# Second cross attention of a two-layer decoder: key tiles in runs of 4, 4, 4, 5 where they went 4, 4, 3, 3, 3

## What is computed

```python
def _L1_xattn_ref(x, latents, key_padding_mask, kv_gate, ...):   # x: ctx (4,1601,256), latents (4,512,256)
    x = layernorm(x, gamma_media, beta_media)
    latents = layernorm(latents, gamma_lat, beta_lat)
    kv = jnp.concatenate((x, latents * kv_gate), axis=1)          # 2113 rows
    q = (latents @ Wq).reshape(b, n, HEADS, DIM_HEAD)             # 8 heads of 64
    k = (kv @ Wk).reshape(b, f + n, HEADS, DIM_HEAD)
    v = (kv @ Wv).reshape(b, f + n, HEADS, DIM_HEAD)
    sim = jnp.einsum('bqhd,bkhd->bhqk', q * SCALE, k)
    sim = sim - jax.lax.stop_gradient(jnp.max(sim, axis=-1, keepdims=True))
    sim = jnp.where(valid_full[:, None, None, :], sim, NEG_INF)
    attn = jax.nn.softmax(sim, axis=-1)
    out = jnp.einsum('bhqk,bkhd->bqhd', attn, v).reshape(b, n, HEADS * DIM_HEAD)
    return out @ Wout
```

## Time and profile before

| | us |
|---|---|
| median of 3 runs | 2297.67 |
| lowest, highest | 2291.8, 2297.82 |
| the profiled execution | 2294.18 |
| its span, first to last instruction | 2292.4 |
| the stage that is touched | about 931 to 1930 in that span |
| granted PE clock over the span (share of full) | 0.944 |

### The profile page before, as it was taken

The page is one execution under the profiler, slowest core; times in us unless marked ns, Lnnn a source line. Parts: engine busy times, 40 slices in busy tenths (PEclk is TensorE's granted clock), DMA queues, the critical chain, the costliest instruction groups (busy, mean ns, idle before and its releaser), DMA issues. The chain is left out here.

```text
span 2292.4 us, 35767 instructions
## 1 busy us (share of the span) xinstructions
PE 2004.5 (87%) x12692; PEld 1395.7 (61%) x12692; DVE 1529.4 (67%) x2457; ACT 1158.6 (51%) x2226; POOL 954.7 (42%) x754
## 2 busy tenths in 40 slices
PE   7898867994989996899999999999999996799992
PEld 4565546993343544566666666665666664699992
DVE  5677864553787887688788778877888886222224
ACT  3332311102367456668775877677776772233332
POOL 2233232322221131166665756575666664222223
PEclk9999978997999997999999999999999997899996
DMA  4100016311000000100000000000000001621113
GB/s 156 39 23 22 23 64 258 101 63 62 0 0 1 0 29 27 40 1 1 30 1 1 10 29 1 1 10 1 1 1 1 10 1 65 250 75 36 38 33 120
DMA packets 36779, 93.30 MB, mean 41 GB/s; under 512 B 5479, under 2 KB 24443, under 8 KB 31998
## 3 DMA queue, kind: packets, MB, share of 16 engines
q1 hardware_dynamic: 30526, 74.72, 9.1%
q0 software_dynamic: 6080, 16.29, 2.1%
HBM read 76.56 MB, written 14.44 MB: 40 GB/s over the span
## 5 line engine op out<-in xcount | busy, mean ns | idle before, releaser
L2052 POOL TENSOR_TENSOR x_total<-x_total,x_pt 128x1024 f32<-128x1024 f32 x189 | 446.5, 2363 | 171.4 <-ACT x_pt L2138 153.6
L2160 ACT ACTIVATE x_pt<-PS,x_maskf 128x512 f32<-128x512 f32 x544 | 332.1, 689 | 165.0 <-PE PS L2474 163.6
L2259 DVE TENSOR_TENSOR PS<-x_pt,PS 128x512 f32<-128x512 f32 x480 | 333.5, 695 | 64.8 <-ACT x_pt L2160 27.3
L2277 DVE TENSOR_TENSOR x_pt<-x_pt,PS 128x1024 f32<-128x1024 f32 x320 | 320.4, 1053 | 0.7 <-PE PS L2492 0.7
L2474 PE MATMUL PS<-x_qs,x_ks 64*128 64x256 f32 x2176 | 281.9, 396 | 1.5 <-ACT x_pt L2160 1.5
L2451 PE MATMUL PS<-x_pt,x_vs 128*64 128x256 f32 x2108 | 262.7, 388 | 20.6 <-issue 12.1
L2138 ACT ACTIVATE x_pt<-x_pt 128x1536 f32<-128x1536 f32 (+1 forms) x160 | 266.5, 1667 | 12.8 <-DVE x_pt L2277 12.8
L2474 PEld LDWEIGHTS PS<-x_qs,x_ks 64*128 64x128 f32 x2176 | 199.6, 189 | 64.5 <-issue 39.0
L1143 PEld LDWEIGHTS PS<-m_xT,m_own 128*128 128x128 f32 x1984 | 234.5, 195 | 6.9 <-DVE m_own L1219 2.9
L1143 PE MATMUL PS<-m_xT,m_own 128*128 128x128 f32 x1984 | 235.4, 278 | 2.8 <-DVE m_own L1219 2.4
L2451 PEld LDWEIGHTS PS<-x_pt,x_vs 128*64 128x64 f32 x2108 | 141.8, 137 | 137.2 <-issue 67.5
(11 more groups left out here) (301 smaller groups left out, 2832.1 us busy)
## 6 DMA issues: line engine op xcount, KB each, us to landing
f_w<-in_L_ffn_w SPq DMA_DIRECT2D x32, 1024.0 KB, 6.5
a_ctxT<-in_ctxT SPq DMA_DIRECT2D x8, 800.5 KB, 4.3
f_w<-ys SPq DMA_DIRECT2D x24, 256.0 KB, 5.4
l_w<-in_ctx SPq DMA_DIRECT2D x4, 1024.0 KB
l_w<-in_L_attn_w SPq DMA_DIRECT2D x6, 512.0 KB, 7.6
a_xT<-in_xT SPq DMA_DIRECT2D x4, 512.0 KB, 5.8
X<-in_x SPq DMA_DIRECT2D x1, 2048.0 KB, 11.1
xr<-a_xn SPq DMA_DIRECT2D x16, 128.0 KB, 1.7
```

The lines of the kernel that those rows point to most:

```text
L2052: ins = nc.gpsimd.tensor_tensor(total2[:], first, tile[:, 2 * k + 2:2 * k + 4, :], ALU.add)
L2160: nc.scalar.activation(pt[:, s % 2, t, :].rearrange("p (h n) -> p h n", h=2), PS[:, first:first + 2, half], ACT.Identity, bias=maskf[:, b ...
L2259: ins = nc.vector.tensor_tensor(acc, tile, acc, ALU.max)
L2277: nc.vector.tensor_tensor(p_, p_, PS[:, MB, None, :].to_broadcast([P, at.stop - at.start, SPAN]), ALU.subtract).then_inc(lowered, 1)
```

## The change

The steps become four, with 4, 4, 4 and 5 tiles. The fills of keys and values no longer follow the runs: they have boundaries of their own (`CUTS`), 4, 4, 4, 4 and 1 tiles, so there are still five K and five V fills. The fifth K fill (one tile) is made in step 1 of an even slot, the fifth V fill (one tile) in step 3 of an even slot, both behind `weigh`. The fourth K fill is made where the fifth was. The pieces that DVE lowers are eight of two tiles and one of one tile, where they were seven of two and three of one. N fills, ten in slots i = 5 and 6, go 1, 2, 1, 1 and 1, 1, 2, 1 to a step (`TURNS`), where each step had one. O goes to steps 1 and 2 where it had 2 and 4; x and L stay in steps 1 and 3. The statistics are spread over 11 steps where it was 14, and ACT's normalising over 9 steps.

```diff
-    NG = 5
-    EDGES = [0, 4, 8, 11, 14, KT]
+    NG = 4
+    EDGES = [0, 4, 8, 12, KT]
+    CUTS = [0, 4, 8, 12, 16, KT]
+    NF = len(CUTS) - 1
+    FILLED = [range(CUTS[i], CUTS[i + 1]) for i in range(NF)]
...
-    PIECES = [(0, 2), (2, 4), (4, 6), (6, 8), (8, 10), (10, 11), (11, 13), (13, 14), (14, 16), (16, KT)]
+    PIECES = [(0, 2), (2, 4), (4, 6), (6, 8), (8, 10), (10, 12), (12, 14), (14, 16), (16, KT)]
...
-    SUMMED = [1, 3, 5, 6, SUMS]
+    SUMMED = [1, 3, 5, SUMS]
...
+        TURNS = {(0, 0): 1, (0, 1): 2, (0, 2): 1, (0, 3): 1, (1, 0): 1, (1, 1): 1, (1, 2): 2, (1, 3): 1}
+        BEFORE = {at: sum(n for other, n in TURNS.items() if other < at) for at in TURNS}
+
+        def last_cut(gi):
+            return gi if gi < NG - 1 else NF - 1
...
                     made += [("K", b, p, NG - 1)] if gi == 0 and s > 0 else []
                     made.append(("V", b, p, gi))
+                    made += [("K", b, p, NF - 1)] if gi == 1 and s > 0 else []
+                    made += [("V", b, p, NF - 1)] if gi == NG - 1 else []
...
-                at = (i - TURN_SLOT) * NG + gi
-                if b + 1 < B and 0 <= at < KD * len(CGROUPS):
-                    made.append(("N", b + 1) + divmod(at, KD))
+                at = (i - TURN_SLOT, gi)
+                if b + 1 < B and at in TURNS:
+                    made += [("N", b + 1) + divmod(n, KD) for n in range(BEFORE[at], BEFORE[at] + TURNS[at])]
             if b >= 1:
-                if i == 2 and gi in (2, 4):
-                    made.append(("O", b - 1, gi // 2 - 1))
+                if i == 2 and gi in (1, 2):
+                    made.append(("O", b - 1, gi - 1))
...
-                pool.wait_ge(exp_done, u * NG + (1, 2, 2, 3, 4, 4, 5, 5, 5)[k])
+                pool.wait_ge(exp_done, u * NG + (1, 2, 2, 3, 3, 4, 4, 4, 4)[k])
...
-                    if exists(s) and s // UB + 1 < B and s % UB in (3, 4):
+                    if exists(s) and s // UB + 1 < B and s % UB in (3, 4, 5):
...
-            STATS = {at: range(at * NS // 14, (at + 1) * NS // 14) for at in range(14)}
+            STATS = {at: range(at * NS // 11, (at + 1) * NS // 11) for at in range(11)}
...
-                        for k in {1: range(0, 3), 2: range(3, 6), 3: range(6, 8), 4: range(8, 10)}.get(gi, ()):
+                        for k in {1: range(0, 3), 2: range(3, 6), 3: range(6, 9)}.get(gi, ()):
```

More of the change, by code:

```diff
@@ L1864, in layer1_cross @@
         TURN_SLOT = 5
-        PURE = sum(e <= S2 // P for e in EDGES[1:])
+        PURE = sum(e <= S2 // P for e in CUTS[1:])
+        TURNS = {(0, 0): 1, (0, 1): 2, (0, 2): 1, (0, 3): 1, (1, 0): 1, (1, 1): 1, (1, 2): 2, (1, 3): 1}
+        BEFORE = {at: sum(n for other, n in TURNS.items() if other < at) for at in TURNS}
+        def last_cut(gi):
+            return gi if gi < NG - 1 else NF - 1
         def unit(u):
@@ L1888, in uses @@
                     made += [("K", 0, 0, c) for c in range(PURE)] + turns(0, len(CGROUPS) - 1)
-                    made += [("q", 0, 0)] + [("K", 0, 0, c) for c in range(PURE, NG)]
+                    made += [("q", 0, 0)] + [("K", 0, 0, c) for c in range(PURE, NF)]
                 return made
@@ L1953, in key_cols @@
         def key_cols(c):
-            return slice(EDGES[c] * P, EDGES[c + 1] * P)
+            return slice(CUTS[c] * P, CUTS[c + 1] * P)
         def piece_of(t):
@@ L2108, in move @@
                 elif use[0] == "V":
-                    ts = TILES[use[3]]
+                    ts = FILLED[use[3]]
                     ins = nc.scalar.copy(vs[:, use[2] % 2, ts.start:ts.stop, :],
@@ L2169, in _ @@
                                 normalise(s // UB + 1, k)
-                    if UB <= s < UNITS and s % UB == 3 and gi == 4:
+                    if UB <= s < UNITS and s % UB == 3 and gi == NG - 1:
                         b = s // UB
@@ L2400, in fill @@
                     pe.wait_ge(gated, b + 1)
-                    for i, t in enumerate(TILES[c]):
+                    for i, t in enumerate(FILLED[c]):
                         for k in range(KD):
@@ L2463, in scores @@
                         b, p, hq = unit(s)
-                        released(pe, ("K", b, p, gi))
+                        released(pe, ("K", b, p, last_cut(gi)))
                         released(pe, ("q", b, p))
@@ L2519, in _ @@
                 pe.wait_ge(exp_done, u * NG + gi + 1)
-                released(pe, ("V", b, p, gi))
+                released(pe, ("V", b, p, last_cut(gi)))
                 for t in TILES[gi]:
```

2 lines of the change are left out of this document (1 added, 1 removed).

## The result

| | median us | lowest, highest | runs |
|---|---|---|---|
| before | 2294.71 | 2291.23, 2299.67 | 13 |
| changed | 2300.87 | 2297.69, 2306.09 | 13 |

The ratio is 1.0025, with a 95% interval of 1.0016 to 1.0034: the change makes the kernel slower by 6.2 us. The forecast was 2307.2, 9.5 us above the median shown then. The direction held, the size did not: the forecast lies 12.5 us above the 2294.71 that 13 runs give, and the changed kernel 6.2. Of the 6.3 us between 2307.2 and 2300.87, 3.3 are the size (9.5 against 6.2), and 3.0 are the time it was counted from: the median of three runs, 2297.67. The loss lies just under the 0.3% that was named as the bound, so the outcome is the one that had 0.32, and not the one that had 0.56.

What follows compares the result with a forecast made beforehand. VectorE's gapless chain was taken to bound 18 of 31 slots, PE the other 13. Terms 3 + 5.9 + 2 - 0.4 - 1.3 gave +9.2, called +9.5 with the longer last exponential: median 2307.2 us, 8-in-10 range 2294 to 2322.

Steps and rivals of the forecast that it cites:

- VectorE's chain sets the plain slots: In 18 of 31 slots VectorE runs some 24.5 us without a gap, so PE's saved time there becomes idle time.
- Slot i = 6, +5.9: Three PE-bound slots with N fills: new waits outweigh saved work, +2.0 us each, +5.9 together.
- the third piece: Last scores run, tiles 12 to 16: PE waits for banks ScalarE must empty, 0.7 us, or 1.7 in slot 6.
- N to N: Wait of an N fill right behind another N fill, for ScalarE's copy out of the one bank: +0.55 us.
- s: PE time to fill one tile of keys or values; not in the trace, taken as 0.6 us, upper end 0.86.
- Slot i = 2, +2: Three PE-bound slots with O fills: work nearly even, added waits make +0.7 us each, +2 together.
- VectorE's slots, +3: The 18 slots VectorE bounds: +0.15 us each for its chain, +0.1 in nine odd ones; +3, range 0 to +7.
- i = 4, -0.4: Three PE-bound slots with x and L fills: waits removed and added nearly balance, -0.4 us together.
- i = 5, -1.3: Four PE-bound slots: K fill and other PE work shrink, waits roughly even, -1.3 us together.
- the clock: Rival, 0.13: longer PE waits drop PE to 1.2 GHz, 1.6 us each, +21 us in all, giving 2328.
- The small fills ride free: Rival, 0.20: ScalarE's copies finish in time and small fills add almost no waits; about +2 us, 2299.7.
- PE is the bound: Rival, 0.12: PE limits the kernel after all, so its full 17.6 us saving comes through, giving 2280.1.

## Where the prediction held, and where it failed

- *VectorE's chain sets the plain slots, PE's saving turns into waiting*: right. 24.64 without a gap (24.67 forecast), period 27.19, PE waits 1.20 ahead of the turning (1.6 expected). The kernels without the division show it by cutting the chain.
- *Slot i = 6, +5.9*: measured +5.7, by errors of both signs. The waits came out smaller: the third piece has 1.46 (forecast 1.7), N to N 0.50 (0.55), K to N 0.36 (0.45), V to N 0.35 (0.45) and 0.14 (0.4), together 2.8 where 3.55 was forecast. The matmuls came out dearer by about as much: V, `weigh`, scores and K were forecast to change by -0.03 in sum, and a four-tile V fill behind scores takes 1.98 where 1.88 was taken, the 17th tile's scores 0.64 where 0.43 was, and s came to 0.64, taken as 0.6.
- *Slot i = 2, +2*: measured +2.1, and +2.9 without the lower clock that had reached into slots 10 and 18 before.
- *VectorE's slots, +3*: measured +1.8. The lower clock that left slots 9 and 17 (1.9) and came in 30 and 31 (1.75) nearly cancels, so +2.0 without it. The odd ones are twelve, where the sum counts nine; the five plain ones (7, 15, 23, 25 and 27) have +0.09 to +0.14, where 0.25 was forecast, and slots 3, 11 and 19 have -0.25: they lost a wait of 0.29 in VectorE's chain. In the plain even ones a cost was missed: the small K fill in step 1 was taken as PE time with room in the slot, when the step had 0.3 and the fill takes 0.64; slot 24 has +0.57 instead of 0.15. Slack was counted per slot and had to be counted per step.
- *i = 4, -0.4*: measured -3.3. Of that 3.1 are lower clock that left slot 20, against 1.6 that came in slot 12; -1.8 without it. The third piece, the K to x and the V to L waits are there (0.50, 0.36 and 0.35 in slot 20), and the late V move is smaller than taken: 0.18 ahead of the small V fill. This term was 1.4 too high. (Its parts, as the prediction gives them, add up to 0.0 and not to -0.4.)
- *i = 5, -1.3*: measured -2.8, of which 1.6 are the stretch that left slot 21; -1.2 without it.
- *The step that failed is the clock, which the sum 3 + 5.9 + 2 - 0.4 - 1.3 takes at nothing.* It stood as a rival only, and as a loss: more spare time on PE, more stretches. It had the wrong sign. The waits of 1.2 ahead of the turning brought none in the plain odd slots; between the first and the last reduction the stretches went from seven to three, worth -4.0, and one came behind, worth +1.7. In sum -2.3 of the 6.6 that the traces differ by, and most of the distance to 9.5.
- *The rest of the sum*: the slots without the clock come to +7.6, where the working had +9.2. Slot 0 has +1.3, which the working doesn't have: the same two kinds of wait, 0.68 and 0.50. The end has +0.2 besides the clock, where 0.3 was allowed for the longer exponential. So the mechanisms come to 9.1 where 9.5 was forecast, with an i = 4 term 1.4 too high and slot 0 left out, which nearly cancel. That is luck in the sum, and not precision. With the clock, and 0.2 that the changed kernel's trace is ahead when the stage begins, it is the measured 6.6.
- *The base* was off too: of the 6.3 us between forecast and result, 3.0 are the median of three runs that the forecast was counted from.
- *The small fills ride free*, given 0.20: refuted by the kernel with only those, 1.0037.
- *PE is the bound*, given 0.12: refuted by the pair without the division.
- Slower by over 0.3% had 0.56, within 0.3% had 0.32; 0.25% with an interval up to 0.34% is the second.
- *What stays open*: why a given wait is followed by the lower clock in one batch and not in the next.
